# Adapters fed from a second, token-last copy of x; first FFN step prepared by blocks of 128 rows with filler matmuls; eight expert result buffers

## The chip, the cores and the metric

One core of a Trainium2 chip runs the whole program in one launch. The metric is the device time of that launch in microseconds (us), median over runs, lower is better. The engines are PE (TensorE), DVE (VectorE), ACT (ScalarE), POOL (GpSimd) and SP (SyncE, which here only issues transfers). Each engine works through its own instructions in order and waits on semaphores for the others.

## The reference

Two layers over x of shape (8, 512, 256), float32; 8 samples of 512 tokens, 4096 tokens of width 256.

```
# layer 0, conditioning: one adapter per sample, chosen by language id
h  = relu(x[b] @ W1[lang] + b1[lang])            # 256 -> 64
y  = x[b] + h @ W2[lang] + b2[lang]              # 64 -> 256
n  = (y - mean) * rsqrt(var + 1e-5) * gamma[lang] + beta[lang]
# layer 0, FFN: each of 8 experts takes, per sample, its 128 best tokens
S  = softmax(n @ Wg.T); G, I = top_k(S per sample and expert, 128)   # of 512 tokens
o  = gelu(n[I] @ W1e + b1e) @ W2e + b2e          # 256 -> 1024 -> 256
x  = x + scatter_add(G * o)
# layer 1, conditioning: 8 causal exponential averages over the tokens, gates, projections, layernorm
# layer 1, FFN: 64 experts, 8 per token, capacity 128 rows each, plus a shared expert
for e in 64: out[rows(e)] += weight * (silu(z @ gate_e) * (z @ up_e)) @ down_e   # 256 -> 192 -> 256
x  = x + routed + shared
```

In this kernel a step of the first FFN works on 4 samples x 128 chosen tokens = 512 rows of one expert; there are 16 steps, s = 2e + p, with p the half of the samples.

## The kernel before

**Stages.** The program has four stages, and each engine has its own hand-written order of calls: the adapters (8 samples), a selection of the best 128 tokens for each sample and expert, the first FFN (16 steps, a hardware loop over pairs of experts), the conditioning of layer 1 (8 samples, software-pipelined), and the 64 experts of layer 1. Semaphores start at a credit of 12, so `level(m)` is the count reached when item m is done.

**Adapters.** For each sample b SP runs `a_load(b)`: it waits for `a_y` of sample b-2, reads the language id from memory into a register (`value_load`), and issues seven transfers: x rows (512 KB, into one of two buffers `xt`), the adapter's two matrices and biases, and gamma and beta. PE turns x with eight transposes (`a_xT_in`, L1514), ACT copies them from PSUM to the single buffer `xT` (`a_xT_out`, L753), PE computes the hidden layer from it (`a_hidden`, L1523), ACT applies the relu (L758), PE multiplies back (`a_adapted`, L1531), and DVE adds x (L1059) and takes the statistics. POOL computes the reciprocal root, DVE normalises, ACT stores the rows to `n0_rows` and PE transposes them (`a_backT`, L1540) for the router's logits (`a_logits`, L1548). PE's order is: hidden(b), logits(b-2), adapted(b), xT_in(b+1), backT(b-1). `a_hidden` waits on all six small transfers of its sample at once (`a_in`, 6 x 16).

**Selection.** DVE does 16 rounds of max, index and replace on a table that PE transposed (L1570). When it is done (`k_sel`), PE turns values and indices (L1573, L1574), later reverses half of them by a product with `flip` (L1577, L1578), and DVE merges the lists into `idxT` (`k_tab`). PE has nothing to do in between.

**First step of the FFN.** POOL copies four columns of `idxT` to `take` (L583), waits for its own copy, and issues four indirect gathers of 128 rows (L587); all four count into one semaphore, `b_got[0]`. PE waits for all, does eight transposes into banks 0 and 1 (`b_T_in`, L1587), DVE scales them to `ex_raw` (L1166), copies them to the rounded type (L1171) and subtracts (L1173). Then PE starts the matmuls of the step (L1602). Of the numbers on each side, the products use a high and a low part (three matmuls for one).

**Experts.** For each expert e POOL gathers rows (L713) into one of `ROWS = 6` buffers and adds the result rows to memory (`e_scatter`, L720). PE's order in iteration e is gate_up(e) (L1845), hidden_in(e-1) (L1852), rows_in(e+2) (L1837), down(e-2) (L1862), and parts of `prep`, which works out the row lists of four later experts (L1741, L1747, L1752). ACT's order is silu(e), hidden_out(e-1), rows_out(e-2), the last of which writes the result rows into one of four buffers `ys`:

```python
wait_moved(act, e_put[e % 2], e // 2 - 2, 16)      # rows_out: the scatter of e-4 has landed
A.activation(ys[e % 4][:, :], bank[:, 6 + e % 2, H:2 * H], ACT.Copy)
...
wait_moved(pool, e_put[e % 2], e // 2 - 1, 16)     # e_scatter: the scatter of e-2 has landed
```

POOL's order is scatter(e-3), then gather(e+6). Before the loop PE transposes the rows of experts 0 and 1, and DVE runs xgT_out(0), xgT_out(1), prep(1, 2).

Of the kernel before, what the change touches and what calls it, by code (L numbers as in the profile page):

```python
# [14 lines left out]
F32 = mybir.dt.float32  # L15
# [8 lines left out]
P = 128  # L24
# [39 lines left out]
def build(nc, t):  # L64
# [20 lines left out]
    with ctx:  # L85
# [69 lines left out]
        xT = sb("xT", [P, CT, S])  # L155
# [102 lines left out]
        ys = [sb(f"ys{i}", [P, H]) for i in range(4)]  # L258
# [25 lines left out]
        def z_bank(q):  # L284
# [20 lines left out]
        a_x = [sem(f"a_x{p}", 16) for p in range(2)]  # L305
        a_in = [sem(f"a_in{p}", 16 * 6) for p in range(2)]
        a_stored = [sem(f"a_stored{p}", 16) for p in range(2)]
        a_xTm, a_xT, a_hm, a_h, a_ad, a_y, a_mv, a_rstd, a_nrm, a_nT, a_yT, a_lgm, a_lg = (
            sem("a_" + n) for n in ("xTm", "xT", "hm", "h", "ad", "y", "mv", "rstd", "nrm", "nT", "yT", "lgm", "lg"))
# [8 lines left out]
        b_got = [sem(f"b_got{p}", 0) for p in range(2)]  # L318
        b_put = [sem(f"b_put{p}", 0) for p in range(2)]
# [62 lines left out]
        def _(sp):  # L382

            def a_load(b):
                h, p = divmod(b, 2)

                sp.wait_ge(a_y, level(b - 2))
                lang = sp.value_load(t["ids"][0:1, b:b + 1], min_val=0, max_val=LANGS - 1)
                sp.dma_start(xt[p][:, :, :], x_rows[b * S:(b + 1) * S, :].rearrange("(t p) c -> p t c", p=P)).then_inc(a_x[p], 16)
# [3 lines left out]
                sp.dma_start(b1c[p][:, :], t["ab1"][bass.ds(lang, 1), :].rearrange("l a -> a l")).then_inc(a_in[p], 16)  # L393
                sp.dma_start(gam0[:, b, :], t["agam"][bass.ds(lang, 1), :, :].rearrange("l p c -> (l p) c")).then_inc(a_in[p], 16)
# [111 lines left out]
        def _(pool):  # L506
# [82 lines left out]

            def b_put_index(g, r):  # L590
# [56 lines left out]
            b_gather(0, 0)  # L647
# [68 lines left out]
            def e_scatter(e):  # L716
                pool.wait_ge(e_ys, level(e))

                wait_moved(pool, e_put[e % 2], e // 2 - 1, 16)
                G.indirect_dma_start((out, odd_rows)[e % 2][:, :], bass.IndirectOffsetOnAxis(ap=slots[:, e:e + 1], axis=0),  # L720
                                     ys[e % 4][:, :], None, compute_op=ALU.add).then_inc(e_put[e % 2], 16)
# [21 lines left out]
        def _(act):  # L743
# [6 lines left out]
            def a_xT_out(b):  # L750
                act.wait_ge(a_xTm, level(b))
                act.wait_ge(a_hm, level(b - 1))
                A.activation(xT[:, :, :], two(0), ACT.Copy).then_inc(a_xT, 1)  # L753

# [18 lines left out]
            a_xT_out(0)  # L773
            for b in range(B):
                a_front(b)
                if b + 1 < B:
                    a_xT_out(b + 1)
# [256 lines left out]
            def rows_out(e):  # L1034
                act.wait_ge(e_d, level(e))

                wait_moved(act, e_put[e % 2], e // 2 - 2, 16)
                A.activation(ys[e % 4][:, :], bank[:, 6 + e % 2, H:2 * H], ACT.Copy).then_inc(e_ys, 1)  # L1038
# [11 lines left out]
        def _(dve):  # L1050
# [5 lines left out]
            def a_front(b):  # L1056
                p = b % 2
                dve.wait_ge(a_ad, level(b))
                V.tensor_tensor(y[p][:, :, :], rows4(3), xt[p][:, :, :], ALU.add).then_inc(a_y, 1)  # L1059
# [142 lines left out]
            b_exT_out(0, 0)  # L1202
# [298 lines left out]
        def _(pe):  # L1501
# [6 lines left out]
            def a_xT_in(b):  # L1508
                p = b % 2
                pe.wait_ge(a_x[p], level(b // 2, 16))  # L1510
                pe.wait_ge(a_xT, level(b - 1))
                for c in range(CT):
                    for j in range(TT):
                        o = T.transpose(bank[:, c, j * P:(j + 1) * P], xt[p][:, j, c * P:(c + 1) * P], ident[:, :])  # L1514
                o.then_inc(a_xTm, 1)

            def a_hidden(b):
                p = b % 2
                pe.wait_ge(a_in[p], level(b // 2, 16 * 6))
                pe.wait_ge(a_xT, level(b))  # L1520
                pe.wait_ge(a_h, level(b - 1))
                for c in range(CT):
                    o = T.matmul(bank[0:AD, 2, :], w1c[p][:, c, :], xT[:, c, :], start=(c == 0), stop=(c == CT - 1))  # L1523
# [28 lines left out]
            a_xT_in(0)  # L1552
            for b in range(B):
# [4 lines left out]
                if b + 1 < B:  # L1558
                    a_xT_in(b + 1)
# [11 lines left out]
            o.then_inc(k_pT, 1)  # L1571
# [363 lines left out]
```

## Time and profile before

| | |
|---|---|
| time, median of 3 runs | 1130.76 us (1129.94 to 1133.33) |
| profiled execution, its own time | 1128.04 us |
| its span, first to last instruction | 1126.3 us |
| PE busy | 939.8 us (83%) |
| POOL busy | 663.5 us (59%) |
| DVE busy | 743.0 us (66%) |
| ACT busy | 470.3 us (42%) |
| mean granted TensorE clock | 0.911 of full speed |

Busy time is no bound by itself: the stages have different limits. The granted clock has two levels in this trace, 0.5 (1.2 GHz) and 1.0 (2.4 GHz); values between are windows that hold both. Start times are counted from the first instruction.

### The profile page before, as it was taken

What the parts mean: (1) busy time and instruction counts of PE and PEld (TensorE: products, weight loads), DVE (VectorE), ACT (ScalarE), POOL (GpSimd) and SP (SyncE); (2) the same over time, 40 slices, a digit from 0 to 9 for tenths busy, and PEclk for the clock granted to TensorE, in tenths of its full rate; (3) what the DMA queues carried; (4) which work ended last, traced back from release to release, by engine and by line L of the source; (5) the groups of instructions that cost most, each with busy time, mean ns of one, the idle gap of its engine ahead of it and who ended that gap; (6) DMA issues with size and microseconds to landing.
All of it is one profiled execution on the core that took longest, in us unless ns stands there. A gap on an engine that the chain in (4) does not pass through costs nothing. (4 is left out here: it accounts for less than half of the span.)

```text
span 1126.3 us, 15057 instructions
## 1 busy us (share of the span) xinstructions
PE 939.8 (83%) x4616; PEld 676.5 (60%) x4616; DVE 743.0 (66%) x1523; ACT 470.3 (42%) x843; POOL 663.5 (59%) x495
## 2 busy tenths in 40 slices
PE   5981399999999999988478899998777798999960
PEld 3761289998999899973134555554454465556540
DVE  3547366766676667534578999999874786777620
ACT  2331055445544555354346665666422132233320
POOL 1113415545554555325899999999850577777870
PEclk9885599999999999998689999999876999999995
DMA  2559514444443443223212652344348599997558
GB/s 78 149 185 368 157 47 90 94 117 86 89 96 77 120 90 52 29 57 108 86 51 75 214 159 87 111 136 119 104 140 317 172 254 254 270 260 152 94 72 157
DMA packets 90455, 151.28 MB, mean 134 GB/s; under 512 B 15816, under 2 KB 72848, under 8 KB 87248
## 3 DMA queue, kind: packets, MB, share of 16 engines
q1 hardware_dynamic: 55184, 95.46, 25.9%
q0 software_dynamic: 25104, 39.86, 20.5%
q10 hardware_dynamic: 10096, 15.10, 4.1%
q8 instruction: 33, 0.54, 0.2%
q14 instruction: 38, 0.31, 0.1%
HBM read 115.37 MB, written 43.42 MB: 141 GB/s over the span
## 5 line engine op out<-in xcount | busy, mean ns | idle before, releaser
L628 POOL TENSOR_TENSOR wide<-wide 128x1024 f32<-128x1024 f32 x64 | 156.5, 2459 | 32.1 <-issue 32.1
L1239 DVE TENSOR_TENSOR_SCAN wide<-bank,wide 128x512 f32<-128x512 f32 x128 | 149.4, 1209 | 21.8 <-POOL wide L628 21.8
L855 ACT ACTIVATE h_raw<-bank,b 128x512 f32<-128x512 f32 x128 | 87.9, 688 | 168.3 <-PE bank L1602 165.9
L1194 DVE TENSOR_TENSOR h_lo<-h_raw,h_hi 128x512 fp32r<-128x512 f32 x128 | 87.2, 692 | 93.9 <-ACT h_hi L859 93.9
L1617 PE MATMUL bank<-w_hi,h_hi 128*128 128x256 f32 x512 | 144.3, 282 | 0.1
L1617 PE MATMUL bank<-w_lo,h_hi 128*128 128x256 f32 x512 | 142.1, 277 | 0.0
L1617 PE MATMUL bank<-w_hi,h_lo 128*128 128x256 f32 x512 | 142.0, 277 | 0.0
L602 POOL DMA_INDIRECT x_rows<-ob,put x64 | 110.9, 1733 | 27.3 <-issue 14.3
L636 POOL TENSOR_TENSOR wide<-wide 128x1024 f32<-128x1024 f32 x46 | 108.5, 2358 | 11.9 <-issue 8.2
L879 ACT ACTIVATE wide<-wide,blend 128x512 f32<-128x512 f32 x128 | 84.1, 716 | 59.9 <-POOL wide L628 56.5
L1602 PE MATMUL bank<-ex_hi,w_hi 128*128 128x512 f32 x256 | 100.3, 392 | 4.9 <-issue 4.9
L1602 PE MATMUL bank<-ex_hi,w_lo 128*128 128x512 f32 x256 | 101.3, 396 | 0.0
L1602 PE MATMUL bank<-ex_lo,w_hi 128*128 128x512 f32 x256 | 101.0, 394 | 0.0
L1617 PEld LDWEIGHTS bank<-w_hi,h_hi 128*128 128x128 f32 x512 | 96.8, 189 | 1.6 <-issue 1.1
L1617 PEld LDWEIGHTS bank<-w_lo,h_hi 128*128 128x128 f32 x512 | 96.9, 189 | 0.3 <-issue 0.2
L1617 PEld LDWEIGHTS bank<-w_hi,h_lo 128*128 128x128 f32 x512 | 96.7, 189 | 0.0
L713 POOL DMA_INDIRECT xg<-z_rows,slots x64 | 63.5, 992 | 54.1 <-DVE slots L1377 36.1
L596 POOL COPY put<-idxT 128x4 int32<-128x4 int32 (+1 forms) x16 | 3.0, 185 | 137.8 <-DVE ob L1183 137.8
L587 POOL DMA_INDIRECT xg<-n_rows,take x64 | 67.4, 1052 | 28.2 <-issue 14.9
L859 ACT ACTIVATE h_hi<-h_raw 128x512 fp32r<-128x512 f32 x128 | 77.9, 621 | 0.0
L1038 ACT ACTIVATE ys<-bank 128x256 f32<-128x256 f32 x64 | 24.5, 383 | 98.0 <-DMA out<-ys,slots 43.3
L720 POOL DMA_INDIRECT odd_rows<-ys,slots x32 | 51.4, 1606 | 17.3 <-ACT ys L1038 8.2
(230 smaller groups left out, 2034.1 us busy)
## 6 DMA issues: line engine op xcount, KB each, us to landing
wide<-in_mwp SPq DMA_DIRECT2D x40, 512.0 KB, 4.4
wide<-m_rows SPq DMA_DIRECT2D x16, 1024.0 KB, 4.8
w1s<-in_fW SPq DMA_DIRECT2D x8, 1024.0 KB, 5.0
w2s<-in_fW SPq DMA_DIRECT2D x8, 1024.0 KB, 5.3
own<-in_mwp SPq DMA_DIRECT2D x15, 512.0 KB, 4.2
z_rows<-zrow SPq DMA_DIRECT2D x8, 640.0 KB, 7.1
head<-in_mwp SPq DMA_DIRECT2D x9, 512.0 KB, 4.4
xt<-in_x SPq DMA_DIRECT2D x8, 512.0 KB, 3.9
```

The costliest lines, as they stand in the source:

```text
L587: G.indirect_dma_start(xg0[p][:, j, :], None, n0_rows[:, :], bass.IndirectOffsetOnAxis(ap=take[p][:, j:j + 1], axis=0)).then_inc(b_got[p], 16)
L602: G.indirect_dma_start(x1_rows[:, :], bass.IndirectOffsetOnAxis(ap=put[p][:, j:j + 1], axis=0), ob[p][:, j, :], None, compute_op=ALU.add). ...
L628: G.tensor_tensor(drive[n % DRIVES], gb[d % 2], md[d // HD][:, d % HD, :].unsqueeze(1).to_broadcast([P, CT, S]), ALU.mult).then_inc(c_u, 1)
L636: G.tensor_tensor(acc[b % 2][:, :, :], acc[b % 2][:, :, :], trace[((D - 1) * b + d - 1) % TRACES], ALU.add).then_inc(c_add, 1)
L713: G.indirect_dma_start(xg1[i][:, :], None, z_rows[:, :], bass.IndirectOffsetOnAxis(ap=slots[:, e:e + 1], axis=0)).then_inc(e_got[i], 16)
L855: A.activation(h1_raw[f % 4][:, :], bank[:, 2 + f % 4, :], ACT.Gelu_apprx_tanh, bias=b1_0[:, bass.ds(e, 1), f]).then_inc(b_h, 1)
L859: A.activation(h1_hi[:, f - 1, :], h1_raw[(f - 1) % 4][:, :], ACT.Copy).then_inc(b_hi, 1)
L879: o = A.activation(gb[d % 2][:, c, :], gated2[b % 2][:, c, :], ACT.Copy, scale=blend[:, c, d:d + 1])
L1194: V.tensor_tensor(h1_lo[:, f, :], h1_raw[f % 4][:, :], h1_hi[:, f, :].bitcast(F32), ALU.subtract).then_inc(b_lo, 1)
L1239: o = V.tensor_tensor_scan(dst[:, c, :], decay[:, d:d + 1].to_broadcast([P, S]), drive[(D * b + d) % DRIVES][:, c, :], 0.0, ALU.mult, ALU.add)
L1602: o = T.matmul(bank[:, 2 + f % 4, :], w[q][:, at], x[p][:, c, :], start=(c == 0 and n == 0), stop=(c == CT - 1 and n == 2))
L1617: o = T.matmul(rows4(6)[:, j, :], x[:, f, rows], w[q][:, f * H:(f + 1) * H], start=(f == 0 and n == 0), stop=(f == FT0 - 1 and n == 2))
```

## The change

Three parts, made together. First, the adapters read x a second time from an input that the host wrote with tokens last, into two buffers `xT`; the transposes, the ACT copy and their semaphores go, and the row copy of x is issued later in `a_load`. Second, the gathers of the first FFN step take their indices straight from `idxT`, each with its own semaphore; PE transposes and DVE splits block by block; and PE runs filler matmuls (`turn`) during the selection and between the blocks. The matmuls of the step itself still wait for all four blocks. Third, `ys` has eight buffers, so rows_out(e) waits for the scatter of e-8, and PE transposes the rows of expert 1 after gate_up(0).

```diff
-        xT = sb("xT", [P, CT, S])
+        xT = [sb(f"xT{p}", [P, CT, S]) for p in range(2)]
-        ys = [sb(f"ys{i}", [P, H]) for i in range(4)]
+        ys = [sb(f"ys{i}", [P, H]) for i in range(8)]
...
                 sp.wait_ge(a_y, level(b - 2))
+                sp.dma_start(xT[p][:, :, :], t["xT"][b, :, :].rearrange("(c p) s -> p c s", p=P)).then_inc(a_xin[p], 16)
                 lang = sp.value_load(t["ids"][0:1, b:b + 1], min_val=0, max_val=LANGS - 1)
-                sp.dma_start(xt[p][:, :, :], x_rows[b * S:(b + 1) * S, :].rearrange("(t p) c -> p t c", p=P)).then_inc(a_x[p], 16)
...
+                sp.dma_start(xt[p][:, :, :], x_rows[b * S:(b + 1) * S, :].rearrange("(t p) c -> p t c", p=P)).then_inc(a_x[p], 16)
                 sp.dma_start(gam0[:, b, :], t["agam"][bass.ds(lang, 1), :, :].rearrange("l p c -> (l p) c")).then_inc(a_in[p], 16)
...
+            def b_gather_first():
+                for j in range(4):
+                    G.indirect_dma_start(xg0[0][:, j, :], None, n0_rows[:, :],
+                                         bass.IndirectOffsetOnAxis(ap=idxT[:, j, 0:1], axis=0)).then_inc(b_first[j], 16)
...
-            b_gather(0, 0)
+            b_gather_first()
+            pool.sem_inc(b_take, 1)
...
-                                     ys[e % 4][:, :], None, compute_op=ALU.add).then_inc(e_put[e % 2], 16)
+                                     ys[e % 8][:, :], None, compute_op=ALU.add).then_inc(e_put[e % 2], 16)
...
-            def a_xT_out(b):
-                act.wait_ge(a_xTm, level(b))
-                act.wait_ge(a_hm, level(b - 1))
-                A.activation(xT[:, :, :], two(0), ACT.Copy).then_inc(a_xT, 1)
...
-                wait_moved(act, e_put[e % 2], e // 2 - 2, 16)
-                A.activation(ys[e % 4][:, :], bank[:, 6 + e % 2, H:2 * H], ACT.Copy).then_inc(e_ys, 1)
+                wait_moved(act, e_put[e % 2], e // 2 - 4, 16)
+                A.activation(ys[e % 8][:, :], bank[:, 6 + e % 2, H:2 * H], ACT.Copy).then_inc(e_ys, 1)
...
+                dve.wait_ge(a_x[p], level(b // 2, 16))
                 V.tensor_tensor(y[p][:, :, :], rows4(3), xt[p][:, :, :], ALU.add).then_inc(a_y, 1)
...
+            def b_exT_first():
+                for j in range(4):
+                    at = slice(j * P, (j + 1) * P)
+                    if j < 3:
+                        dve.wait_ge(b_T0, j + 1)
+                    else:
+                        dve.wait_ge(b_T, level(0))
+                    for c in range(CT):
+                        o = V.tensor_scalar(ex_raw[:, c, at], bank[:, (0, 1, 6, 7)[j], c * P:(c + 1) * P], gam0[:, j, c:c + 1], bet0[:, j, c:c + 1],
+                                            ALU.mult, ALU.add)
+                    if j == 3:
+                        o.then_inc(b_xraw, 1)
+                    dve.drain()
+                    V.tensor_copy(ex_hi[0][:, :, at], ex_raw[:, :, at])
+                    dve.drain()
+                    o = V.tensor_tensor(ex_lo[0][:, :, at], ex_raw[:, :, at], ex_hi[0][:, :, at].bitcast(F32), ALU.subtract)
+                o.then_inc(b_exT, 1)
...
-            def a_xT_in(b):
-                p = b % 2
-                pe.wait_ge(a_x[p], level(b // 2, 16))
-                pe.wait_ge(a_xT, level(b - 1))
-                for c in range(CT):
-                    for j in range(TT):
-                        o = T.transpose(bank[:, c, j * P:(j + 1) * P], xt[p][:, j, c * P:(c + 1) * P], ident[:, :])
-                o.then_inc(a_xTm, 1)
...
-                pe.wait_ge(a_xT, level(b))
+                pe.wait_ge(a_xin[p], level(b // 2, 16))
...
+            def turn(n, count):
+
+                for _ in range(count):
+                    T.matmul(bank[:, n, :], ident[:, :], flip[:, :].unsqueeze(1).to_broadcast([P, 4, P]), start=True, stop=True)
+
+            turn(5, 25)
+
             pe.wait_ge(k_sel, 1)
...
-                        b_T_in(s + 1, 1 - p, 2 * g + (r + 1) // 2)
+                        b_T_in(s + 1, 1 - p, 2 * g + (r + 1) // 2 - p)
...
+            def b_T_first():
+                turn(5, 3)
+                for j in range(4):
+                    pe.wait_ge(b_first[j], 16)
+                    for c in range(CT):
+                        o = T.transpose(bank[:, (0, 1, 6, 7)[j], c * P:(c + 1) * P], xg0[0][:, j, c * P:(c + 1) * P], ident[:, :])
+                    o.then_inc(b_T0 if j < 3 else b_T, 1)
+                    turn(5, 1)
...
             rows_in(0)
-            rows_in(1)
             for e in range(E1 + 2):
                 if e < E1:
                     gate_up(e)
+                if e == 0:
+                    rows_in(1)
```

## Rows read from the trace of the kernel before

**Rows 1.** Windows: length, busy PE, PEld, DVE, ACT, POOL, clock, DMA share, GB/s.

```profile
50.00:51.00 1.00, 1.00 (x7) 1.00 (x6) 0.91 (x2) 0.00 (x0) 0.00 (x0) 0.50 0.00 0
...
110.00:112.00 2.00, 0.00 (x0) 0.00 (x0) 1.78 (x8) 0.00 (x0) 0.00 (x0) 0.50 1.01 412
...
140.00:170.00 30.00, 30.00 (x185) 26.70 (x184) 18.24 (x29) 18.31 (x32) 5.83 (x5) 1.00 0.19 45
```

**Rows 2.** Timeline of PE and DVE, adapters: start, us, instruction, idle before.

```profile
11.41 3.65 PE L1523 MATMUL bank<-xT,w1c 128*64 128x512 f32 x4 [1.16 <-issue]
...
42.67 1.04 PE L1540 MATMUL bank<-ident,nrm 128*128 128x128 f32 x8
...
43.99 1.90 PE L1523 MATMUL bank<-xT,w1c 128*64 128x512 f32 x4 [0.29 <-issue]
...
45.82 1.95 PE L1548 MATMUL bank<-wg,yT 128*128 128x8 f32 x16
...
47.63 1.97 PE L1531 MATMUL bank<-w2c,hT 65*128 65x256 f32 x8
...
49.64 1.23 DVE L1059 TENSOR_TENSOR y<-bank,xt 128x1024 f32<-128x1024 f32 x1 [1.43 <-PE bank L1531]
...
68.25 1.90 PE L1523 MATMUL bank<-xT,w1c 128*64 128x512 f32 x4 [0.29 <-issue]
```

**Rows 3.** Timeline of SP's issues for sample 6: first and last of seven.

```profile
52.92 0.39 SPq L389 DMA_DIRECT2D xt<-in_x  x1
...
56.63 0.38 SPq L395 DMA_DIRECT2D bet<-in_abet  x1
```

**Rows 4.** Timeline of PE around the selection.

```profile
91.25 0.66 PE L1570 MATMUL bank<-ident,prob 128*128 128x128 f32 x2 [3.48 <-DVEq L1118]
...
116.45 0.48 PE L1573 MATMUL bank<-ident,gval 128*128 128x128 f32 x1 [24.54 <-DVEq L1131]
```

**Rows 5.** Timeline of the first step of the FFN.

```profile
121.30 1.28 POOL L587 DMA_INDIRECT xg<-n_rows,take  x1 [0.94 <-POOL take L583]
...
125.41 0.95 POOL L587 DMA_INDIRECT xg<-n_rows,take  x1 [0.30 <-issue]
...
128.27 1.94 PE L1587 MATMUL bank<-ident,xg 128*128 128x128 f32 x8 [9.47 <-issue]
...
130.25 2.65 DVE L1166 TENSOR_SCALAR ex_raw<-bank,gam,bet 128x128 f32<-128x128 f32 x8 [10.32 <-PE bank L1587]
...
135.08 0.76 PE L1602 MATMUL bank<-ex_hi,w_hi 128*128 128x512 f32 x1 [4.87 <-issue]
...
138.21 0.51 PE L1602 MATMUL bank<-ex_lo,w_hi 128*128 128x512 f32 x1
...
141.08 0.39 PE L1602 MATMUL bank<-ex_lo,w_hi 128*128 128x512 f32 x1
```

**Rows 6.** Timeline of POOL: the scatters of experts 4, 45 and 55.

```profile
906.53 1.59 POOL L720 DMA_INDIRECT out<-ys,slots  x1 [0.30 <-issue]
...
1047.67 1.59 POOL L720 DMA_INDIRECT odd_rows<-ys,slots  x1 [0.30 <-issue]
...
1079.52 1.59 POOL L720 DMA_INDIRECT odd_rows<-ys,slots  x1 [0.30 <-issue]
```

**Rows 7.** Waits by line, 880 to 1110: total us, times, longest.

```profile
PE bank L1852 <- ACT ys L1038: 9.3, 15, 1.6
```

**Rows 8.** Line L389, the loads of the x rows.

```profile
DMA to landing us min/median/max: 3.6/3.9/5.4
```

**Rows 9.** DMA issues, 0 to 80: KB each, median us to landing.

```profile
b<-in_fb ACTq DMA_DIRECT2D x1, 32.0 KB, 2.1
```

**Rows 10.** Timeline of PE at the first experts.

```profile
877.39 1.53 PE L1845 MATMUL bank<-own,xgT 128*128 128x384 f32 x4 [0.46 <-issue]
...
880.25 0.41 PE L1752 MATMUL bank<-Rx,sel 32*128 32x131 bf16 x4 [1.05 <-DVE sel L1360]
```

**Rows 11.** Line L720, the scatters of all 64 experts.

```profile
DMA to landing us min/median/max: 3.7/4.8/7.4
```

More of the change, by code:

```diff
@@ L305, in build @@
         a_x = [sem(f"a_x{p}", 16) for p in range(2)]
+        a_xin = [sem(f"a_xin{p}", 16) for p in range(2)]
         a_in = [sem(f"a_in{p}", 16 * 6) for p in range(2)]
         a_stored = [sem(f"a_stored{p}", 16) for p in range(2)]
-        a_xTm, a_xT, a_hm, a_h, a_ad, a_y, a_mv, a_rstd, a_nrm, a_nT, a_yT, a_lgm, a_lg = (
-            sem("a_" + n) for n in ("xTm", "xT", "hm", "h", "ad", "y", "mv", "rstd", "nrm", "nT", "yT", "lgm", "lg"))
+        a_hm, a_h, a_ad, a_y, a_mv, a_rstd, a_nrm, a_nT, a_yT, a_lgm, a_lg = (
+            sem("a_" + n) for n in ("hm", "h", "ad", "y", "mv", "rstd", "nrm", "nT", "yT", "lgm", "lg"))
         credits = [len(credited)]
@@ L318, in build @@
         b_got = [sem(f"b_got{p}", 0) for p in range(2)]
+        b_first = [sem(f"b_first{j}", 0) for j in range(4)]
+        b_T0 = sem("b_T0", 0)
         b_put = [sem(f"b_put{p}", 0) for p in range(2)]
@@ L771, in a_store @@
                 act.dma_start(n0_rows[b * S:(b + 1) * S, :].rearrange("(t p) c -> p t c", p=P), nrm[p][:, :, :]).then_inc(a_stored[p], 16)
-            a_xT_out(0)
             for b in range(B):
                 a_front(b)
-                if b + 1 < B:
-                    a_xT_out(b + 1)
                 if b:
@@ L1200, in b_group @@
                             w_lo(2 * g + q + 1, 1 - q, p == 0, n)
-            b_exT_out(0, 0)
+            def b_exT_first():
[15 more added lines that the diff above has]
+                o.then_inc(b_exT, 1)
+            b_exT_first()
             ffn(dve, b_group)
@@ L1519, in a_hidden @@
                 pe.wait_ge(a_in[p], level(b // 2, 16 * 6))
-                pe.wait_ge(a_xT, level(b))
+                pe.wait_ge(a_xin[p], level(b // 2, 16))
                 pe.wait_ge(a_h, level(b - 1))
                 for c in range(CT):
-                    o = T.matmul(bank[0:AD, 2, :], w1c[p][:, c, :], xT[:, c, :], start=(c == 0), stop=(c == CT - 1))
+                    o = T.matmul(bank[0:AD, 2, :], w1c[p][:, c, :], xT[p][:, c, :], start=(c == 0), stop=(c == CT - 1))
                 o.then_inc(a_hm, 1)
@@ L1550, in a_logits @@
                 o.then_inc(a_lgm, 1)
-            a_xT_in(0)
             for b in range(B):
@@ L1557, in _ @@
                 a_adapted(b)
-                if b + 1 < B:
-                    a_xT_in(b + 1)
                 if b:
@@ L1819, in row_0 @@
                     soma_in(0)
-            b_T_in(0, 0, 0)
+            def b_T_first():
[6 more added lines that the diff above has]
+                    turn(5, 1)
+            b_T_first()
             ffn(pe, b_group)
@@ L1920 @@
             a = a.T
+        elif layout == "tokens last":
+            a = a.swapaxes(1, 2)
         elif layout == "columns":
```

2 rows, old and new, of the table LAYOUT are left out of this document.

## The prediction

> **What bounds the kernel now.** I read the busy time by windows first, to learn which stage has which limit, then the timeline of each stage that the change touches, and the waits of the last stage. The first FFN is bound by PE at full clock: in 30 us of it PE is busy for all 30, clock 1.00 [rows 1]. Whatever is won before the FFN starts is therefore kept to the end of it, and the conditioning behind it starts from its last result. So the question ahead of the FFN is only when its first matmul can start, now at 135.08 [rows 5].
>
> The adapters take about 8 us a sample: the hidden layer of sample 0 starts at 11.41, that of sample 7 at 68.25, so (68.25 - 11.41)/7 = 8.12 [rows 2]. PE is busy nearly all that time, but what sets the pace is a ring through several engines: transposes of x, ACT's copy, hidden, relu, second product, next transposes. A second ring runs through memory. The loads of sample b start when y of sample b-2 is done: y of sample 4 ends at 49.64 + 1.23 = 50.87 [rows 2], SP's first issue for sample 6 is at 52.92 (the language id is read in between) and the seventh ends at 56.63 + 0.38 = 57.01 [rows 3].
>
> In the selection PE turns a table at 91.25 and then has nothing until 116.45, idle for 24.54 [rows 4], while DVE works; the clock stands at 0.50, 1.2 GHz [rows 1]. The first step then runs strictly in turn [rows 5]: POOL copies indices and waits 0.94 for its own copy, gathers from 121.30 to 126.36, PE transposes at 128.27, DVE works from 130.25, PE starts at 135.08, slowly: eight matmuls by 138.21 (0.39 each), then 12 by 141.08 (0.24 each), when the clock is back.
>
> In the experts POOL issues a scatter and a gather each. From expert 45 to 55 the ten intervals take 1079.52 - 1047.67 = 31.85, 3.185 each, with gaps of 0.30 only: POOL is the limit. From expert 4 to 45 they take (1047.67 - 906.53)/41 = 3.44 [rows 6]: something holds it back. The waits show ACT on landed scatters and PE on ACT, but of PE only 9.3 us in all [rows 7].
>
> **The adapters.** Gone from PE's order: eight transposes like those of L1540, 1.04 at full clock, and the wait for ACT's copy. What stays is hidden 43.99 to 45.82, logits to 47.63 and eight matmuls of 1.97, then 1.04 of transposes [rows 2]: 1.83 + 1.81 + 1.97 + 1.04 = 6.65 a sample. That would save 8.12 - 6.65 = 1.47 a sample if the memory ring allowed it. It hardly does. SP now has eight issues and the register read in series. From y's end to the first issue of the old order it took 2.05, seven issues took 4.09, 0.58 each [rows 2, 3]. New: 2.05 + 0.5 for the xT issue + four small ones (2.3) put the issue of the x rows at 4.9 after y, and gamma and beta right behind it, the last starting at 6.0. The trace has no small transfer behind a large one. Low: it lands as the lone small one did, 2.1 after its issue [rows 9], at 8.15. High: it comes after the x rows and these take the longest seen, 5.4, at 10.3. I take the x rows' median, 3.9 [rows 8], at 8.8, because the small ones are issued behind 512 KB in the same queue. From hidden's start to y's end is 50.87 - 43.99 = 6.88 [rows 2], so two samples take 6.88 + 8.8 + 0.1 = 15.8, one 7.9 (low 7.5, high 8.6). Against 8.12 over seven samples that is 1.5 won; the first sample also loses its transposes and copy, and is then held by its own small transfers, worth about 1.1: an estimate, since eight cold transposes took 1.94 at L1587 [rows 5] and the copy about 1 behind them, and the later landing takes back two of these three. Together 2.5, from 7 x (8.12 - 8.6) + 1.1 = -2.3 to 7 x (8.12 - 7.5) + 1.1 = 5.4. The x rows themselves are needed 5.6 after hidden starts and come in time. ACT's copies hide behind PE already and are worth nothing beyond this.
>
> The Trainium skill (DMA: Bandwidth & Descriptors, Queues, rings and completion order) says that a transfer's semaphore increment lands only after every earlier write of that DMA engine. By it gamma and beta count as arrived no earlier than the x rows issued ahead of them, which speaks against this order of issue and would give 8.8 or more; no row of before has this case.
>
> **Filler in the selection.** 25 calls on 512 float32 columns are 50 matmuls, as the four of one hidden layer are two calls. At full clock one starts every 0.46 at most (1.83/4) and twice as fast as at half clock, where four took 3.65; with the tail of the last taken off that is 0.86 cold and 0.43 warm [rows 2]. The clock came back 3.1 after the FFN started [rows 5], so: 3.1 us at 0.86 are 4 matmuls, 46 x 0.43 to 0.46 are 19.8 to 21.2, in all 22.9 to 24.3. PE is free from 91.9 to 116.45, 24.5 [rows 4]. It just fits: cost nothing, and the selection's later transposes run warm, a gain of a few tenths that I leave out.
>
> **The first step by blocks.** The index copy and its wait go: first gather at 120.2 instead of 121.30. Gathers start every (125.41 - 121.30)/3 = 1.37, and PE got the last 2.86 after its start [rows 5]. So block 0 is there at about 123.2 (its issue is 0.3 longer) and block 3 at 124.3 + 2.9 = 127.2. DVE's work on four blocks is 135.0 - 130.25 = 4.75, a quarter 1.2, the low bound; split, each block has its own drains and fixed parts, at most 1.6; I take 1.5. From block 0: 123.2 + 0.3 + 4 x 1.5 = 129.5; from block 3: 127.2 + 0.3 + 1.5 = 129.0. The first matmul goes at 129.7, 5.4 earlier. DVE, not PE, is last: between blocks PE has one filler call, 0.9, and two transposes, 0.26, less than DVE's 1.5, so the fillers are hidden. The three calls ahead of block 0 take 2.6 from 120.0 at full clock, hidden too; at half clock 5.2, and block 0 starts 2.0 late. If the clock is up at the start, 19 matmul intervals that took 6.0 take 19 x 0.23 = 4.4, 1.6 more. Sum 7.0, less 0.5 for a mixed clock in front: 6.5. Low end, clock at half all through: a block on PE costs 1.72 + 0.5 = 2.2, more than DVE, the last block is turned at 125.2 + 3 x 2.2 + 0.5 = 132.3, the matmul goes at 133.9, only 1.2 won. High end 7.5. ACT loads its Gelu table behind the first result either way and stays ahead of PE's four banks.
>
> **Experts.** Eight buffers can win at most the distance to POOL's floor: 41 x (3.44 - 3.185) = 10.5, and PE's waits for ACT were 9.3 [rows 6, 7]. But POOL still issues scatter e only when scatter e-2 has landed. Landing takes 4.8 in the median and up to 7.4 [rows 11]; over the part where weights are still loaded it is nearer 6, an estimate between the two, and with some 0.7 from landing to the next issue a pair takes 6.7, 3.35 each. That leaves 41 x (3.44 - 3.35) = 3.7; I take 3. Against it: the rows of expert 1 are now transposed behind gate_up(0), 1.4 to 1.5 long, from 877.39. DVE scales them before it does the counting that PE already waits 1.05 for at 880.25 [rows 10], so that wait, the list of experts 4 to 7 and POOL's gathers behind it come 1.5 later (0 to 2). Net 1.5, from -2 to 10.5.
>
> **Sum.** 2.5 + 6.5 + 1.5 = 10.5. On the profiled execution, 1128.04 with a span of 1126.3, that gives 1117.5 and a span of 1115.8; the median of the runs is 2.7 above that execution, so 1120.3.
>
> **Rivals.**
> *The clock does not come up under the fillers.* Then 50 matmuls take 50 x 0.86 = 43 instead of 24.5 and the selection's next transpose is 18.5 late. With the low end of the blocks (1.2) and the rest as forecast (4.0): 1130.8 + 18.5 - 5.2 = 1144. Fillers overrun from 24.5/0.43 - 50 = 7 matmuls at half clock on, about 6 us; the change loses when the overrun passes what else is won, 5 to 10 us. For it: the clock fell in the adapters to 0.50 with PE busy 1.00 [rows 1]. Against it: it came back in 3.1 under matmuls, and holds through the FFN. 6 in 100.
> *The memory ring is the bound of the adapters, and the experts gain nothing.* Adapters -1, experts -1.5, blocks 5.5: 3.0 won, 1127.8. For it: the sum of issues above and landings up to 5.4. 20 in 100 for something of this size, 1124.5 to 1129.
> *Both rings open.* PE's own 6.65 holds, or the clock no longer falls: adapters 5.4, experts 5, blocks 6.5: 17 won, 1114. For it: POOL kept 3.185 for ten scatters [rows 6]; against it, the landing times. 24 in 100 for 1112 to 1117. The Trainium skill (TensorE: Matmul & The Clock Gate, PE-mode transpose) says that transposes do not count as busy for the clock. By it taking them out would not cool PE and would favour this case; the low clock at 50 to 51, in a stretch of such transposes [rows 1], agrees.
>
> **How the numbers follow.** The forecast case, 1117 to 1124.5, has 48 in 100; above 1129 I leave 8, of which the filler rival has 6. The range 1113 to 1128 takes in the bounds of adapters and experts and leaves out about 2 in 10. A change of 0.3%, 3.4 us, is what can be told from none: faster than 1127.4 has 0.82, the same 0.10, slower than 1134 0.08.
>
> **What the profile of after would show.** Hidden of sample 7 near 65.5; the last issue of a load some 6.6 behind y's end, and PE idle ahead of hidden. 50 filler matmuls ending before the table's result, clock 1.00 from their fourth on. The step's first matmul 9.5 after the first gather's issue, where it was 135.08 - 121.30 = 13.8. Scatters 4 to 45 at 3.35 to 3.4 each, ACT no longer waiting on landings, POOL waiting on the scatter of e-2. Wrong would be: fillers that end after the selection, block times on DVE over 1.7, or landings that grow with the second copy of x.

## The result: slower, 1145.97 us

The changed kernel takes 1145.97 us in the median of four runs (1142.17 to 1152.38), the kernel before, on the same chips, 1130.35. The ratio is 1.0117 (1.0081 to 1.0152). The forecast was 1120.3. The profiled execution took 1142.17, its span is 1140.3, 14.0 longer than before.

First the timeline of the changed kernel, adapters, cut to the loads of samples 4 and 6 and what stands around them. hidden(b), y(b) and so on are the hidden layer and y of sample b:

```profile
11.92 3.64 PE L1535 MATMUL bank<-xT,w1c 128*64 128x512 f32 x4 [11.92 <-DMA bet<-in_abet]
...
39.15 1.22 DVE L1062 TENSOR_TENSOR y<-bank,xt 128x1024 f32<-128x1024 f32 x1 [2.03 <-PE bank L1543]
...
40.40 0.39 SPq L391 DMA_DIRECT2D xT<-in_xT  x1
...
44.53 0.38 SPq L393 DMA_DIRECT2D w1c<-in_aW  x1
...
47.95 0.38 SPq L399 DMA_DIRECT2D bet<-in_abet  x1
...
52.33 3.37 PE L1535 MATMUL bank<-xT,w1c 128*64 128x512 f32 x4 [4.56 <-DMA bet<-in_abet]
...
60.04 1.23 DVE L1062 TENSOR_TENSOR y<-bank,xt 128x1024 f32<-128x1024 f32 x1 [2.23 <-PE bank L1543]
...
61.29 0.39 SPq L391 DMA_DIRECT2D xT<-in_xT  x1
...
65.38 0.39 SPq L393 DMA_DIRECT2D w1c<-in_aW  x1
...
68.80 0.38 SPq L399 DMA_DIRECT2D bet<-in_abet  x1
...
73.52 3.67 PE L1535 MATMUL bank<-xT,w1c 128*64 128x512 f32 x4 [5.16 <-DMA bet<-in_abet]
77.12 3.58 PE L1560 MATMUL bank<-wg,yT 128*128 128x8 f32 x16
80.56 3.76 PE L1543 MATMUL bank<-w2c,hT 65*128 65x256 f32 x8
84.11 1.92 PE L1552 MATMUL bank<-ident,nrm 128*128 128x128 f32 x8
```

The hidden layer of sample 7 starts at 85.95 (it is the instruction behind the last row), against 68.25 in [rows 2]: 17.7 late. Read the chain of sample 4 from y(2)'s end at 40.37: the first load is out 0.03 later, but the second, w1c, only 4.13 behind it. Between the two stands the read of the language id. Beta goes out at 47.95, hidden(4) starts at 52.33, 4.38 later, and what ended PE's wait is beta's transfer. Then the clock: the four matmuls of a hidden layer took 1.90 to 2.08 before in all samples but the first (3.65), here 3.4 to 3.7 in six of eight. Behind hidden(6) PE never idles, and the sample takes 85.95 - 73.52 = 12.43, with every group at nearly twice its length in [rows 2].

PE's waits in the stretch 0 to 110 (total, times, longest); 11.9 of it is the start, the other three are 11.2:

```profile
PE bank L1535 <- DMA bet<-in_abet: 23.1, 4, 11.9
```

Windows of the changed kernel (columns as in [rows 1]); PE is done at 47.77 and stands still until 52.33. The clock is still 1.00 from 49 to 51 and is down to half before PE works again (0.50 from 52 to 52.5). It is back at 1.00 from 56 to 58, falls to 0.50 by 59 with PE busy all the time, in the products of L1543, is up again from 63, falls once more in the wait ahead of hidden(6), and stays at half through sample 6:

```profile
49.00:51.00 2.00, 0.00 (x0) 0.00 (x0) 1.03 (x6) 0.25 (x1) 0.63 (x2) 1.00 1.02 309
51.00:53.00 2.00, 0.67 (x1) 0.29 (x2) 1.33 (x4) 0.00 (x0) 0.63 (x1) 0.71 1.00 369
53.00:55.00 2.00, 2.00 (x4) 0.46 (x2) 0.05 (x1) 0.00 (x0) 0.00 (x0) 0.50 0.31 78
...
59.00:60.00 1.00, 1.00 (x4) 0.71 (x3) 0.00 (x0) 0.00 (x0) 0.00 (x0) 0.50 0.00 0
...
79.00:81.00 2.00, 2.00 (x9) 2.00 (x10) 0.19 (x1) 0.00 (x0) 0.00 (x0) 0.50 0.99 385
```

The selection and the first FFN step, PE's timeline of the changed kernel, which answers to [rows 4, 5]:

```profile
110.92 0.66 PE L1579 MATMUL bank<-ident,prob 128*128 128x128 f32 x2 [3.55 <-DVEq L1121]
111.38 24.27 PE L1585 MATMUL bank<-flip,ident 128*128 128x512 f32 x50
136.10 0.33 PE L1590 MATMUL bank<-ident,gval 128*128 128x128 f32 x1 [0.45 <-DVEq L1134]
...
150.39 0.47 PE L1619 MATMUL bank<-ex_hi,w_hi 128*128 128x512 f32 x1 [2.23 <-issue]
...
151.44 0.63 PE L1619 MATMUL bank<-ex_hi,w_hi 128*128 128x512 f32 x1
...
154.35 0.40 PE L1619 MATMUL bank<-ex_lo,w_hi 128*128 128x512 f32 x1
```

The 50 fillers end in time: from the table to the index transposes 25.18, before 25.20. From there to the first matmul of the step it is 14.29, before 18.63: 4.34 won. DVE's four blocks and the gathers behind it, first and last:

```profile
143.87 0.73 DVE L1213 TENSOR_SCALAR ex_raw<-bank,gam,bet 128x128 f32<-128x128 f32 x2 [4.64 <-PE bank L1843]
...
149.87 0.43 DVE L1220 TENSOR_TENSOR ex_lo<-ex_raw,ex_hi 128x256 fp32r<-128x256 f32 x1
```

```profile
139.57 1.28 POOL L596 DMA_INDIRECT xg<-n_rows,idxT  x1 [19.32 <-DVEq L1150]
...
143.67 0.94 POOL L596 DMA_INDIRECT xg<-n_rows,idxT  x1 [0.30 <-issue]
```

And the scatters of experts 4 and 45, which answer to [rows 6]: 138.08 apart, before 141.14, while the first experts lose as much.

```profile
923.26 1.59 POOL L730 DMA_INDIRECT out<-ys,slots  x1 [0.30 <-issue]
...
1061.34 1.59 POOL L730 DMA_INDIRECT odd_rows<-ys,slots  x1 [0.31 <-issue]
```

Put end to end, after minus before: hidden(7) +17.7, table of the selection +19.7, first matmul of the FFN +15.3, first expert gather +13.4, scatter 4 +16.7, scatter 45 +13.7, end +14.0. The loss is in the adapters.

### The profile page after: what moved, and what is told of

It reads as the page before. It is cut to its first block, busy times and chain, and to the rows that moved or that the text cites. A ratio compares the mean times of both kernels' runs of the same rounds, so it can differ in the third digit from the quotient of the medians.

```text
span 1140.3 us, 15052 instructions
## 1 busy us (share of the span) xinstructions
PE 970.7 (85%) x4616; PEld 688.1 (60%) x4616; DVE 743.9 (65%) x1529; ACT 461.4 (40%) x835; POOL 663.4 (58%) x494
## 4 chain that ended last, share of the span: by engine, by line
POOL 11%; issue 10%; PE 9%; DMA 8%; DVE 7%; ACT 2%; DVEq 2%; POOLq 1%; ACTq 0%; SPq 0%
POOL wide L637 4%; PE bank L1646 4%; POOL wide L645 3%; DMA odd_rows<-ys,slots 3%; DMA xg<-z_rows,slots 3%; DVE wide L1260 2%; POOL xg L723 2%; DMA out<-ys,slots 1%; POOL odd_rows L730 1%; DMA z_rows<-zrow 1%; PE bank L1871 1%; POOL out L730 1%; ACT wide L881 1%; PE bank L1713 1%; ACT zrow L931 1%
## 5 line engine op out<-in xcount | busy, mean ns | idle before, releaser
L591 POOL DMA_INDIRECT xg<-n_rows,take x60 | 63.0, 1050 | 26.1 <-issue 13.7
L730 POOL DMA_INDIRECT odd_rows<-ys,slots x32 | 52.2, 1633 | 17.7 <-issue 5.9
L1028 ACT ACTIVATE sg<-bank 128x192 f32<-128x192 f32 x64 | 21.2, 331 | 98.9 <-PE bank L1871 98.9
```

## The experiments

The runs in one table; times in us from the profiled execution of each, the ratio to the kernel before on the same chip, where its median was 1130.4 to 1132.8. "hidden(7)" and "table" are start times, "idx to FFN" is from the index transposes to the first matmul of the first step.

| kernel | hidden(7) | table | idx to FFN | gather 0 to scatter 4 | scatters 4 to 45 | median, ratio (95%) |
|---|---|---|---|---|---|---|
| before | 68.25 | 91.25 | 18.63 | 34.4 | 141.1 | 1130.35 |
| after | 85.95 | 110.92 | 14.29 | 37.8 | 138.1 | 1145.97, 1.0117 (1.0081 to 1.0152) |
| adapters_only | 89.94 | 114.92 | 18.97 | 34.7 | 140.8 | 1153.0, 1.0186 (1.0112 to 1.0261) |
| without_adapters | 72.22 | 94.93 | 15.21 | 37.8 | 141.7 | 1131.02, 0.9958 (0.9914 to 1.0001) |
| id_first | 74.35 | 97.02 | 15.57 | 35.6 | 142.1 | 1135.25, 1.0032 (0.9999 to 1.0065) |
| rows_last | 78.36 | 103.34 | 14.43 | 36.6 | 142.9 | 1140.47, 1.005 (1.001 to 1.009) |
| id_ahead_rows_last | 66.55 | 89.03 | 14.32 | 34.6 | 141.3 | 1121.81, 0.9919 (0.9886 to 0.9953) |
| fill_adapters | – | – | – | – | – | 1142.88, 1.0088 (1.0043 to 1.0133) |
| second_copy_unused | 85.19 | 107.91 | 18.61 | 33.7 | 142.0 | 1143.64, 1.0107 (1.0038 to 1.0177) |
| blocks_no_fill | 68.07 | 91.18 | 14.62 | 35.2 | 140.5 | 1125.51, 0.997 (0.9936 to 1.0004) |
| no_fill_old_experts | 60.99 | 83.49 | 14.74 | 34.3 | 140.7 | 1119.26, 0.9896 (0.9856 to 0.9937) |
| id_ahead_alone | 67.20 | 90.25 | 18.59 | 33.5 | 141.7 | 1133.3, 0.9994 (0.9966 to 1.0021) |
| second_copy_last | 70.09 | 92.49 | 18.74 | 34.2 | 141.3 | 1129.71, 0.9982 (0.9957 to 1.0006) |
| experts_only | 68.97 | 91.38 | 18.72 | 35.3 | 138.7 | 1137.02, 1.0047 (1.0019 to 1.0076) |

One trace stands behind each row, and the same code does not give the same times. With the adapters of before unchanged hidden(7) starts between 68.07 and 72.22 (before, without_adapters, blocks_no_fill, experts_only); after and adapters_only, 85.95 and 89.94, have the same adapters; so have id_ahead_rows_last and no_fill_old_experts, 66.55 and 60.99. Differences of 4 to 6 us at hidden(7) or at the table are therefore within what one trace can vary.

**The parts apart.** adapters_only is the kernel before with the first part of the change alone, without_adapters has the other two.

> The kernel before with only the adapters' part of the change. If the whole loss lies in the adapters (hidden layer of sample 7 at 85.95 instead of 68.25 after the change, and the table of the selection 19.7 later), this takes 19 to 20 us more than before, about 1150, and PE idles ahead of hidden on the transfer of beta. Rival, that the loss needs the fillers or the blocks as well (heat, or the clock spent in the selection): under 1140.

> The change with the adapters of before. If the adapters are the whole loss: the blocks keep the 4.0 us seen (first matmul of the FFN 15.3 late where the table was 19.3 late), experts about 0, so 1124 to 1127. Rival, that fillers or experts lose too: 1130 or more.

The adapters alone cost 1.9%, hidden(7) is 21.7 late, as expected. The rest alone took 1131.02, not 1124 to 1127; that is the number of the rival, but the kernel before took 1132.82 on that chip, so no loss shows: by the interval it is worth at most 0.9%, and nothing at its other end. So the adapters are the whole loss, within these intervals.

**The order of SP's issues.** id_first is the changed kernel with the id read ahead of the first large transfer, but still behind the wait on y:

```diff
                 sp.wait_ge(a_y, level(b - 2))
+                lang = sp.value_load(t["ids"][0:1, b:b + 1], min_val=0, max_val=LANGS - 1)
                 sp.dma_start(xT[p][:, :, :], t["xT"][b, :, :].rearrange("(c p) s -> p c s", p=P)).then_inc(a_xin[p], 16)
-                lang = sp.value_load(t["ids"][0:1, b:b + 1], min_val=0, max_val=LANGS - 1)
```

rows_last leaves the id where the change put it and issues the rows of x behind gamma and beta:

```diff
-                sp.dma_start(xt[p][:, :, :], x_rows[b * S:(b + 1) * S, :].rearrange("(t p) c -> p t c", p=P)).then_inc(a_x[p], 16)
                 sp.dma_start(gam0[:, b, :], t["agam"][bass.ds(lang, 1), :, :].rearrange("l p c -> (l p) c")).then_inc(a_in[p], 16)
                 sp.dma_start(bet0[:, b, :], t["abet"][bass.ds(lang, 1), :, :].rearrange("l p c -> (l p) c")).then_inc(a_in[p], 16)
+                sp.dma_start(xt[p][:, :, :], x_rows[b * S:(b + 1) * S, :].rearrange("(t p) c -> p t c", p=P)).then_inc(a_x[p], 16)
```

> The change, with the language id read before xT is issued, not behind it. After the change SP took 3.1 to 4.1 us from the start of xT's issue to the next issue, where before the read took 2.05 in all. Theory A, the read is slow because 512 KB have just been issued ahead of it: the read falls back to about 2.0, each load ends 1 to 2 us earlier, the ring of two samples shortens by that, four times, and hidden of sample 7 starts 4 to 7 us earlier: 1139 to 1142. Theory B, the clock at 1.2 GHz is the cause and the waits follow from it: same as the change, 1146.

> The change, with the row copy of x issued last, behind gamma and beta. Theory A, the adapter waits because its small transfers land behind the 512 KB of rows: beta's issue to hidden falls from 4.4 to about 2.5 and the issue is 0.6 earlier, 2.5 us a ring, hidden of sample 7 8 to 10 us earlier, 1136 to 1138. Theory B, the clock: same as the change, 1146. Theory C, only the amount moved matters, not its order: also 1146.

Of id_first, SP's timeline for sample 6, whose y(4) ends at 54.47 + 1.23 = 55.70:

```profile
54.47 1.23 DVE L1062 TENSOR_TENSOR y<-bank,xt 128x1024 f32<-128x1024 f32 x1 [2.35 <-PE bank L1543]
...
57.63 0.39 SPq L392 DMA_DIRECT2D xT<-in_xT  x1
58.21 0.38 SPq L393 DMA_DIRECT2D w1c<-in_aW  x1
...
61.60 0.38 SPq L399 DMA_DIRECT2D bet<-in_abet  x1
...
65.31 2.51 PE L1535 MATMUL bank<-xT,w1c 128*64 128x512 f32 x4
```

The read takes 1.93 here, as before, and w1c follows the large transfer by 0.58, where the eight samples of after show 3.10 to 4.15. The read is two loads in turn, and the first can be seen by itself, minimum, median and maximum in ns, in the changed kernel and then in id_first:

```profile
L392 SPq TENSOR_LOAD <-in_ids_ptr x8: 1120/1806/2684, 2.4 to 69.8; - x8
```

```profile
L391 SPq TENSOR_LOAD <-in_ids_ptr x8: 1018/1026/1311, 1.9 to 65.0; - x8
```

Beta is out 5.90 behind y, in after 7.58 and 7.53; hidden(6) is no longer released by it. One moved line gives back 13.9 us at the table, though PE still has the half clock in most samples. hidden(7) came 11.6 earlier, more than the 4 to 7 of theory A, and theory B is refuted; the intervals of id_first and after do not overlap. In rows_last the small transfers no longer stand behind the rows, and from beta's issue to hidden(4) and hidden(6) it takes 2.8 (where PE did not wait for it, so at most) and 3.9 instead of 4.4 and 4.7. But the rows of one sample now go out right ahead of the next sample's id read:

```profile
53.40 0.43 SPq L399 DMA_DIRECT2D xt<-in_x  x1
53.88 0.59 SPq L391 DMA_DIRECT2D xT<-in_xT  x1
...
59.20 0.39 SPq L393 DMA_DIRECT2D w1c<-in_aW  x1
```

Behind 1 MB the read holds SP from 53.88 to 59.20, 5.3. That fits with this run giving back only 7.6 at the table, where more was expected. Its ratio, 1.001 to 1.009, still touches that of after, so by itself it shows a direction and no size. The two edits belong together, and id_ahead_rows_last makes both; the rows move as in rows_last, and the read goes ahead of the wait:

```diff
+                lang = sp.value_load(t["ids"][0:1, b:b + 1], min_val=0, max_val=LANGS - 1)
                 sp.wait_ge(a_y, level(b - 2))
                 sp.dma_start(xT[p][:, :, :], t["xT"][b, :, :].rearrange("(c p) s -> p c s", p=P)).then_inc(a_xin[p], 16)
-                lang = sp.value_load(t["ids"][0:1, b:b + 1], min_val=0, max_val=LANGS - 1)
```

> The change, with the language id read before SP waits for y, xT issued right behind the wait, and the row copy of x last. Theory A (the ring through memory): from y's end to the end of beta's issue it is 0.5 + six issues of 0.58 = 4.0, with landing 6.5 to 7.5, and 7 to 9 for the rest of the ring, so 13.5 to 16 for two samples instead of 20.4 to 21.2; hidden of sample 7 at 58 to 66, total 1116 to 1125. Theory B (the clock alone): hidden of sample 7 stays above 75 and the total above 1135.

1121.81, faster than both kernels and in the range of theory A, with hidden(7) at its upper end. For sample 6 (y(4) ends at 51.91, its timeline, SP and PE) beta is out 4.2 behind y, and PE's hidden layer does not wait for it:

```profile
51.94 0.39 SPq L392 DMA_DIRECT2D xT<-in_xT  x1
...
56.09 0.38 SPq L398 DMA_DIRECT2D bet<-in_abet  x1
...
59.08 1.93 PE L1535 MATMUL bank<-xT,w1c 128*64 128x512 f32 x4
```

**Is it the clock, or the bytes?** fill_adapters is the changed kernel with filler matmuls on PE ahead of hidden, three calls before sample 0 and two before samples 2, 4 and 6, so that PE does not stand still:

> The change, with filler matmuls also in the adapters: three calls ahead of sample 0, two ahead of samples 2, 4 and 6, where PE waits for its transfers. Theory B (the clock is the cause): hidden products fall from 3.6 to 1.9, the ring of two samples loses 2 to 4 us, hidden of sample 7 near 74, total about 1134. Theory A (memory sets the ring, the cold clock adds only what lies between hidden and y, 8.9 instead of 6.9): at most 2 us a ring, 4 to 6 in all, less what the fillers delay: hidden of sample 7 at 80 to 86, total 1140 to 1147.

Its median is 1142.88, ratio 1.0088 (1.0043 to 1.0133), an interval that overlaps that of the changed kernel; theory B's 1134 is outside. Only its timed runs are used, so whether the fillers held the clock is not shown. Fillers in PE's wait do not bring the loss back. second_copy_unused is the kernel before, with the id read first and then the second copy loaded ahead of the rows of x into buffers that nothing is computed from; PE waits for it as well:

```diff
+                sp.dma_start(xU[p][:, :, :], t["xT"][b, :, :].rearrange("(c p) s -> p c s", p=P)).then_inc(a_xin[p], 16)
                 sp.dma_start(xt[p][:, :, :], x_rows[b * S:(b + 1) * S, :].rearrange("(t p) c -> p t c", p=P)).then_inc(a_x[p], 16)
...
+                pe.wait_ge(a_xin[p], level(b // 2, 16))
```

> The kernel before, which loads the token-last copy of x as well (issued behind the id read, ahead of the rows) but does not use it; the transposes stay. Only traffic and one issue are added. Theory A (the place of the read and of the rows does the harm): under 3 us more than before, 1131 to 1134. Theory C (512 KB more a sample is what costs): 8 us or more, above 1139.

In second_copy_last the same copy is issued behind beta instead, nobody on PE waits for it, and SP waits for the copy of b-2 ahead of it:

> The kernel before with the second copy of x loaded behind gamma and beta of each sample and used by nobody; the same bytes as in the run that loads it first. Theory (the order in the queue costs, not the bytes): hidden(7) stays within 3 us of 68.25 and the time within 3 us of 1130.4, where the copy issued first cost 13. Rival (the extra 4 MB take the memory's time away from the other loads and from the stores): hidden(7) at 76 or later, 1138 or more.

The first costs 1.1%, 13 us where its theory A allowed 3: taken alone, that is the number of theory C, the bytes. The second, with the same bytes, costs nothing, which refutes C. PE's waits, 0 to 110, of the one and then of the other:

```profile
PE bank L1517 <- DMA xt<-in_x: 13.1, 4, 9.9
```

```profile
PE bank L1518 <- DMA xt<-in_x: 8.9, 3, 8.3
```

The extra 4 MB fit. What costs is a large transfer ahead of the one that is waited for: the rows of x land 5.3 behind their issue in the median with the copy ahead, 4.2 with the copy last, 3.9 before [rows 8], and PE's added wait on the copy itself appears in no row. The waits differ by only 4.2 us, though, and hidden(7) by 15.1; the larger part is matmuls at half clock, as the table in the next section shows. id_ahead_alone is the kernel before with the read moved ahead of the wait on y:

> The kernel before with one line moved: the language id is read ahead of the wait on y instead of behind it, x in one layout. Theory (the loads' start is on the ring that sets the adapters' pace): the first issue comes 2.05 us sooner after y, three rounds of the ring (samples 2, 4, 6) give up to 6 us if the ring of transposes, ACT's copy and hidden does not hold them: hidden(7) 62 to 67 against 68.25, 1125 to 1129 in all. Rival, the ring through engines sets the pace and memory is hidden: hidden(7) at 68, time unchanged at 1130.4.

No change, 0.9994 (0.9966 to 1.0021), though the loads start 2 us earlier behind y: before the change the adapters did not hang on the memory ring, as the rival had it. The change made them hang on it, and second_copy_unused shows that a large transfer ahead is enough for that, with the transposes in place.

**Blocks and fillers.** blocks_no_fill is the kernel before with the first step by blocks and all filler calls set to zero:

> The kernel before with the block-wise first step and no filler matmuls at all. After the change it was 14.3 from the selection's index transposes to the step's first matmul instead of 18.6. Theory, the blocks alone bring it: 14.5 to 15.5 here too, total 1127. Rival, the fillers bring it: 16.5 to 18.6, since PE's transposes are cold at half clock; total 1129 to 1131.

The step starts 4.0 us earlier with cold transposes and no fillers, against 4.3 in the changed kernel; the time, 0.997 (0.9936 to 1.0004), is not clearly below that of before. PE's timeline there:

```profile
123.50 0.66 PE L1860 MATMUL bank<-ident,xg 128*128 128x128 f32 x2 [4.76 <-DMA xg<-n_rows,idxT]
...
131.01 0.76 PE L1636 MATMUL bank<-ex_hi,w_hi 128*128 128x512 f32 x1 [3.02 <-issue]
```

What the fillers do for the matmuls of the step differs between traces. In id_ahead_rows_last, which has them all, the step runs at full clock from its start:

```profile
128.52 0.47 PE L1619 MATMUL bank<-ex_hi,w_hi 128*128 128x512 f32 x1 [2.24 <-issue]
128.82 0.39 PE L1619 MATMUL bank<-ex_lo,w_hi 128*128 128x512 f32 x1
```

From its first matmul to its twentieth it is 4.42 there, and 6.01 to 6.04 in after, without_adapters, id_first and rows_last, which have the same fillers; before it is 6.00, in blocks_no_fill 6.15.

**Experts.** experts_only is the kernel before with eight buffers and `rows_in(1)` behind gate_up(0):

> The kernel before with eight result buffers and rows_in(1) behind gate_up(0), nothing else. Forecast on record: 1.5 us won, scatters 4 to 45 in 137 to 139. What the runs so far suggest: scatters 4 to 45 in 140.5 to 143 as with four buffers, gather 0 to scatter 4 up to 3 us longer than 34.4, so 0 to 3 us lost, 1130 to 1133.

Waits of POOL and ACT, 880 to 1110, in this run:

```profile
POOL odd_rows L720 <- DMA odd_rows<-ys,slots: 6.8, 6, 1.3
...
ACT ys L1038 <- PE bank L1862: 62.3, 64, 2.2
```

ACT waits on no landed scatter any more, as meant. POOL now waits for the scatter of e-2, and PE waits 2.9 for DVE's `sel` at the first experts, where it was 1.0 [rows 10]. Scatters 4 to 45 are 2.4 shorter, gather 0 to scatter 4 is 0.9 longer; but the median is 1137.02, above the 1130 to 1133 expected and 0.5% slower than before, and the profiled execution, at 1128.82 the fastest of its twelve, does not show where. In after and experts_only scatters 4 to 45 take 138.1 and 138.7; in the four other traces with eight buffers (without_adapters, id_first, rows_last, id_ahead_rows_last) they take 141.3 to 142.9, no less than the 140.5 to 142.0 with four.

**The parts that pay, together.** no_fill_old_experts is id_ahead_rows_last without any filler, with four buffers and `rows_in(1)` at its old place:

> The kernel with the id read ahead of the wait and the rows of x issued last, but without the filler matmuls (both the 25 calls of the selection and the seven of the first step), with four result buffers and rows_in(1) back at its old place. Theory: fillers and the expert part bring nothing, so the time stays at 1118 to 1123 against 1121.8 with them; hidden(7) near 66.6, table near 89, index transposes to first FFN matmul 14.3 to 14.6, gather 0 to scatter 4 back to 34.4 to 35.2 instead of 34.6 to 37.8, scatters 4 to 45 in 140.5 to 141.3. Rival, the fillers do keep the clock and are worth what the forecast gave them: the step takes 1.5 to 2 us more, 1124. Rival, eight buffers bring 3 us and are missed: scatters 4 to 45 in 143 or more.

1119.26, ratio 0.9896 (0.9856 to 0.9937), the lowest of all, but its interval overlaps that of id_ahead_rows_last (0.9886 to 0.9953). So what the fillers and the expert part are worth, either way, is not told apart here. hidden(7) was expected near 66.6 and came at 60.99 with the same adapters: the difference is in the clock (next section). PE's timeline and a window of its adapters:

```profile
46.06 1.93 PE L1535 MATMUL bank<-xT,w1c 128*64 128x512 f32 x4 [0.75 <-DMA bet<-in_abet]
47.92 1.95 PE L1560 MATMUL bank<-wg,yT 128*128 128x8 f32 x16
49.73 1.97 PE L1543 MATMUL bank<-w2c,hT 65*128 65x256 f32 x8
51.54 1.04 PE L1552 MATMUL bank<-ident,nrm 128*128 128x128 f32 x8
53.28 1.93 PE L1535 MATMUL bank<-xT,w1c 128*64 128x512 f32 x4 [0.70 <-DMA bet<-in_abet]
```

```profile
46.00:53.00 7.00, 6.52 (x36) 4.63 (x36) 4.28 (x14) 1.87 (x4) 1.27 (x2) 1.00 0.76 237
```

These are the four groups that took 12.43 in the changed kernel's sample 6; here 7.22, with 0.70 of wait. Beta, issued at 51.48, releases hidden(6) 1.80 later.

## Why the prediction was wrong

Two steps failed. **The first is the memory ring**: "From y's end to the first issue of the old order it took 2.05 ... New: 2.05 + 0.5 for the xT issue". The read was priced as it stood, in a quiet queue, though the change moves it behind a transfer of 512 KB. By the row for sample 4 the time from xT's issue to w1c's is 4.13, of which the issue is 0.58, so the read takes some 3.5. Beta was forecast to start 6.0 behind y; it started 7.6 behind for samples 4 and 6. That is 1.6 of a round, and id_first, where it is 5.9, confirms it.

**The landing of gamma and beta** was forecast 2.8 behind beta's issue (8.8 - 6.0) and took 4.4 and 4.7; the high end, 10.3 from y, would have been 4.3. Together 12.0 and 12.3 from y to hidden instead of 8.8 (10.1 for sample 2). With the rows issued behind beta, PE released by it starts 1.8 to 3.9 behind its issue (rows_last, id_ahead_rows_last, no_fill_old_experts), where it is 3.2 to 4.7 in after. The Trainium skill (DMA: Bandwidth & Descriptors, Queues, rings and completion order) has the semaphore wait for the earlier writes of its DMA engine; the shorter times with the rows issued last agree with it, though they don't prove that mechanism.

**The second is the clock. Hidden to y's end, 6.88 a sample at full clock,** became 8.94 for samples 2 and 4. No term stood for it, since the clock was taken to stay as it was or to gain. Two samples then take 20.9 and 21.2, forecast 15.8. The comparison in the forecast was also uneven: it set 7.9 at full clock against 8.12, an average that has half clock in it. At full clock a sample took 7.65 before (68.25 - 60.60), so even with every other term right the new ring gained nothing there.

How much is wait and how much is clock can be split from the rows of PE between hidden(0) and hidden(7). "Work" takes each group at its length at full clock (1.83, 1.81 and 1.81 for hidden, logits and product, 0.88 for eight transposes), "idle" is what the rows give as idle, and what is left, an estimate, is the cost of half clock:

| kernel | in all | work | idle | half clock |
|---|---|---|---|---|
| before | 56.8 | 46.0 | 4.1 | 6.8 |
| without_adapters | 60.8 | 46.0 | 3.8 | 11.1 |
| second_copy_last | 58.7 | 46.0 | 3.9 | 8.8 |
| second_copy_unused | 72.0 | 46.0 | 6.4 | 19.6 |
| no_fill_old_experts | 52.7 | 39.8 | 5.1 | 7.8 |
| id_ahead_rows_last | 58.2 | 39.8 | 4.8 | 13.6 |
| id_first | 63.0 | 39.8 | 6.3 | 16.9 |
| rows_last | 68.3 | 39.8 | 9.2 | 19.3 |
| after | 74.0 | 39.8 | 12.7 | 21.5 |
| adapters_only | 78.1 | 39.8 | 12.9 | 25.4 |

After against before: 6.2 less work, 8.6 more idle, 14.7 more half clock, in sum the 17.2 that are lost. The larger term is the clock, which the forecast put at nothing. The same adapters code differs in this column by 4 to 6 and in idle by no more than 0.4, so this is also what varies from run to run. More idle time goes with more half clock in the table, but only fill_adapters tried the clock by itself, and its timed runs cannot show whether it held: how much of the clock's fall is due to the waits stays open. The rule weighed in the forecast (the Trainium skill, TensorE: Matmul & The Clock Gate, PE-mode transpose), by which fewer transposes would not cool PE, was no help: the hidden layer ran cold in six of eight samples. Nor is the stretch in [rows 1] evidence for it: in the changed kernel the clock fell to 0.50 by 59 in the products of L1543, before the transposes at 59.80 and without any since 47.77.

**"Both rings open", PE's own 6.65 a sample,** was the right size for PE at full clock: id_ahead_rows_last shows 59.08 - 52.29 = 6.79. It needed another order of issues. The first sample, priced at 1.1 won, began its hidden layer 0.5 later than before, at 11.92.

**Fillers cost nothing:** right, 24.27 for 50, forecast 22.9 to 24.3; the rival that they overrun is refuted. But their gain of 1.6 was not there. The step starts at 150.39, its matmuls soon take 0.63 and from 154.35 on 0.40: the clock fell right behind its start (0.92 from 150 to 151, then 0.50). PE's wait of 2.23 lies ahead of it, but that alone is not the reason: id_ahead_rows_last has a wait of 2.24 there, keeps the clock, and gains just the 1.6. So the term was of the right size and came in one of five traces; why not in the others stays open.

**Blocks:** the first gather came 3.47 behind the index transposes, before 4.85: 1.4 won, forecast 1.1. From there to the first matmul 10.8, forecast 9.5, before 13.8. DVE took 6.43 for four blocks, 1.6 each, the upper bound. The step starts 4.3 earlier, where the forecast had 5.4, and of the 1.6 in the matmuls behind it nothing came; together 6.5 was forecast.

**Experts:** 3 was forecast for scatters 4 to 45, and the trace of after shows 3.1, but four of six traces with eight buffers show none of it. The other side was priced 1.5 (0 to 2) and took 3.4 at the first experts, 0.2 to 3.4 in the six traces. Net nothing, and by the timed runs of experts_only a loss.

In sum: adapters 2.5 won turned into 19.7 lost, blocks 4.3 instead of 6.5, experts 1.5 turned into none; that leaves 15.4, and the 1.4 to the 14.0 at the end is within the few us by which single traces differ.

## What to carry to other kernels

When an issue moves, ask what is in the queue ahead of every instruction that follows, a register read from memory included: read such values before the wait that releases the loads, and issue what is waited for first, large and late-needed transfers last. Work taken off an engine may uncover a ring that it hid, and the waits that appear may come with more work at half clock, here, by the estimate above, 14.7 us of it beside 8.6 of idle time: price the new bound at both clock levels, and the old one at the same level as the new. Keep the part of a change that pays; here the blocks and the token-last copy with another order gave 0.8 to 1.0% where the whole lost 1.2%. And take more than one trace before a few us of a stage are read: the same adapters code moved by 4 to 6.

## What was not expected of the hardware

A read of a value from memory into an SP register takes 1.9 to 2.05 us in a quiet queue, 2.5 to 3.6 right behind a transfer of 512 KB (the 3.10 to 4.15 between issues, less 0.58), and 4.7 behind two. A second copy of x, 4 MB in 60 us, cost 12 us when issued ahead of the rows and nothing behind all else. PE's granted clock was still 1.00 from 49 to 51, where PE stood still; it fell by 52 ahead of the work, and by 59 in the middle of it, with PE busy 1.00 in the products of L1543, as it was with PE busy 1.00 in [rows 1]. It was 0.50 for all of the 12.43 of sample 6. The same adapters code had 7.8 us of half clock in one trace and 13.6 in another.
